# Two cross-attention passes in one kernel: the weighted sums between a step's two blocks of scores

## What is computed

```
q = (queries @ Wq + bq), k = (keys @ Wk + bk), v = (values @ Wv + bv)   # 16 heads of 8
scores = jnp.einsum('bhld,bhsd->bhls', q, k) * SCALE                   # 64 x 6272 a head
weights = jax.nn.softmax(scores, axis=-1)
out = jnp.einsum('bhls,bhsd->bhld', weights, v)
out = out.transpose(0, 2, 1, 3).reshape(B, L, D_MODEL)
out = out @ Wo + bo
```

## Time and profile before

| what | us |
|---|---|
| median of three runs | 349.97 (348.47 to 351.13) |
| the profiled execution | 349.22 |
| its span, first to last instruction | 347.4 |
| PE matmul busy | 305.5 (88%) |
| PE weight loads busy | 208.1 (60%) |
| DVE busy | 223.6 (64%) |
| ACT busy | 168.5 (48%) |
| chain that ended last, on PE | 72% |

### The profile page before, as it was taken

How to read it: one execution, slowest core, us unless ns; L and a number is a source line. 1 busy time by engine, 2 the same in 40 slices (tenths; PEclk the granted TensorE clock), 3 DMA queues, 4 the chain that set the end, 5 groups by cost and what they waited for, 6 DMA issues and landing times.

```text
span 347.4 us, 7751 instructions
## 1 busy us (share of the span) xinstructions
PE 305.5 (88%) x3308; PEld 208.1 (60%) x3308; DVE 223.6 (64%) x452; ACT 168.5 (48%) x224; POOL 30.6 (9%) x22
## 2 busy tenths in 40 slices
PE   2999979999999998998775998999999996647976
PEld 1446747777677774555254665777777775234645
DVE  5588678788875102763996788878878302537653
ACT  2344445556556767593954233655646683012000
POOL 9400000000000012331350000000000000000000
PEclk9999999999999999998899899999999999675999
DMA  7653986544300450201044999954669200000000
GB/s 255 241 113 87 257 185 132 121 93 104 88 2 2 172 219 0 48 15 31 2 91 104 204 347 401 242 130 93 136 222 458 126 2 1 2 0 1 2 0 6
DMA packets 8114, 41.12 MB, mean 118 GB/s; under 512 B 2192, under 2 KB 2512, under 8 KB 7568
## 3 DMA queue, kind: packets, MB, share of 16 engines
q1 hardware_dynamic: 7936, 40.32, 41.1%
q10 hardware_dynamic: 144, 0.31, 0.3%
HBM read 21.32 MB, written 0.03 MB: 61 GB/s over the span
## 4 chain that ended last, share of the span: by engine, by line
PE 72%; DVE 16%; ACT 7%; issue 3%; DMA 1%; POOL 0%; ACTq 0%; DVEq 0%
PE ps L712 71%; ACT prob L342 2%; DVE arena L469 2%; DVE arena L466 2%; DVE mx L441 2%; DVE y L420 1%; DMA consts<-in_const 1%; ACT arena L322 1%; ACT arena L324 1%; DVE arena L475 1%; PE ps L724 0%; PE ps L856 0%; ACT lnv L347 0%; DVE st L416 0%; DVE vaug L701 0%
## 5 line engine op out<-in xcount | busy, mean ns | idle before, releaser
L342 ACT ACTIVATE prob<-ps 128x1024 f32<-128x1024 f32 (+1 forms) x104 | 100.4, 976 | 64.6 <-PE ps L712 64.2
L441 DVE TENSOR_REDUCE mx<-ps 128x1 f32<-128x512 f32 (+1 forms) x156 | 95.2, 655 | 22.8 <-PE ps L712 20.0
L712 PE MATMUL ps<-qst,kst 128*128 128x256 f32 x392 | 71.9, 305 | 2.9 <-DVE qst L436 2.2
L712 PE MATMUL ps<-kst,qst 128*128 128x512 f32 (+1 forms) x208 | 70.6, 416 | 4.4 <-issue 2.9
L712 PEld LDWEIGHTS ps<-qst,kst 128*128 128x128 f32 x392 | 53.8, 188 | 20.4 <-issue 10.1
L712 PE MATMUL ps<-prob,vaug 128*18 128x128 f32 x1568 | 55.8, 274 | 0.0
L712 PEld LDWEIGHTS ps<-kst,qst 128*128 128x128 f32 x208 | 35.4, 189 | 19.9 <-issue 9.3
L712 PEld LDWEIGHTS ps<-prob,vaug 128*18 128x18 f32 x1568 | 40.4, 97 | 11.3 <-issue 8.5
L447 DVE TENSOR_REDUCE mx<-ps 128x2 f32<-128x1024 f32 (+1 forms) x26 | 29.6, 1160 | 7.2 <-PE ps L712 7.1
L307 ACT ACTIVATE vaug<-ps 128x512 f32<-128x512 f32 (+1 forms) x26 | 14.8, 573 | 28.1 <-PE ps L712 27.7
L460 DVE COPY avsb<-ps 128x256 f32<-128x256 f32 x8 | 3.4, 420 | 31.5 <-PE ps L712 31.5
(11 more groups left out here) (190 smaller groups left out, 270.9 us busy)
## 6 DMA issues: line engine op xcount, KB each, us to landing
kst<-arena SPq DMA_DIRECT2D x48, 192.0 KB, 3.2
kst<-arena SPq DMA_DIRECT2D x48, 128.0 KB, 2.4
arena<-in_experts SPq DMA_DIRECT2D x1, 5760.0 KB, 18.6
kst<-arena SPq DMA_DIRECT2D x24, 144.0 KB, 2.7
w<-in_experts SPq DMA_DIRECT2D x1, 3456.0 KB, 11.8
w<-in_late SPq DMA_DIRECT2D x1, 3284.5 KB, 11.5
arena<-in_experts SPq DMA_DIRECT2D x1, 3072.0 KB, 14.3
arena<-in_ctxT SPq DMA_DIRECT2D x2, 768.0 KB, 8.0
```

The lines of the kernel that those rows point to most:

```text
L342: nc.scalar.activation(prob[:, B % PROBS, 0:w], ps[:, b0:b0 + 2, :].rearrange("p a b -> p (a b)")[:, 0:w], ACT.Exp, scale=XSCALE).then_inc ...
L441: V.reduce_max(mx[:, p, k:k + 1], ps[:, bnk, 0:width(k)], AX).then_inc(max_read, 1)
L712: return mm(out_, lhsT, rhs, start=start, stop=stop, skip_group_check=True)
```

## The change

In a step of two blocks, the scores of the first block are now followed by up to two slots, then by the weighted sums of the preceding step, then by the scores of the second block and the rest of the slots. In a step of one block the preceding step's weighted sums now stand first, then the scores and all slots. `gather` and the weights of layer 1 still stand at the end of their step. No other engine's list changes.

```
                     left = list(slots)
-                    for G, i in here:
-                        scores(G, i)
-                        if left:
-                            max_slot(l, left.pop(0))
+                    if len(here) == 2:
+                        scores(*here[0])
+                        for s in left[:2]:
+                            max_slot(l, s)
+                        left = left[2:]
+                    for G, i in before:
+                        weighted(G, i)
+                    scores(*here[-1])
                     for s in left:
                         max_slot(l, s)
-                    for G, i in before:
-                        weighted(G, i)
                     if j == 1 and g >= 1:
                         gather(G0 + g - 1)
```

## The result

The changed kernel took 357.3 us (median of four runs, 354.5 to 360.1) beside 349.3 of the kernel before: a ratio of 1.020, 95% interval 1.015 to 1.025. The longest of the four, 360.1 us, counts as a slow execution and is left out of the ratio; the other three have a median of 356.1. Timed again on another occasion the kernel took 358.5, a ratio of 1.028 (1.024 to 1.031). I had said 354, 350.5 to 356.5, and slower: the sign was right, the size too small by 2 to 4.5 us. The range holds the 356.1, but neither 357.3 nor 358.5. The profiled execution is that longest one (mean granted clock 0.938), so I use it for what happens inside the cross-attentions and have a second profile of the same kernel beside it.

A forecast was written before the change was run, and what follows sets the result against it. Two loops, exponentials and the maxima's banks, were taken to hold full steps near 3.2 us, the banks' remaining after the change. Per layer 0.34 plus 1.9, twice, gave 4.5 us on 349.22 or 349.97: forecast 354, range 350.5 to 356.5.

The forecast's parts named there:

- Two loops: Full cross-attention steps: second block's exponential waiting on a prob buffer (3.20 us) and maxima waiting on three banks (3.19).
- the banks' loop: Full steps: a maximum waits until the bank three slots earlier is read; still 3.19 us a step after the change.
- First steps: Start of layer 0's cross-attention: weighted sums of step [3,4] at 53.26, 1.20 us earlier than before.
- Boundaries: From step [11,12] to the next group's [3,4]: 9.92 us, 1.07 more, with block 0 waiting 0.48 for the accumulator's copy.
- The gather's switch: Four gathers separated from weighted sums: 0.43 instead of 0.23 ahead, already in the sum; another 0.21 each would add 0.8.
- To the last copy: From step [9,10] of group 2 to a layer's last copy: about 22.2 us in layer 1, 1.9 more than 20.34.
- Block 0's wait for its exponential: Group 3: block 0's weighted sums wait for its own exponential, at 7.78 instead of about 7.1, about 0.7 us.
- steps of group 3: Group 3, without maxima: a new loop through each second block's exponential, 2.42 us a step against 2.50.
- The banks' loop not binding: Rival: 18 full steps at 3.06 give back 2.3 us, total 351.6; chance 0.12.
- The exponentials as the whole stall: Rival: waits for exponentials vanish, full steps 3.06, group 3 steps 2.14, total 343; chance 0.06.
- PE full: Rival: order makes no difference, only four gathers' switch is paid, 4 x 0.2, total 350; chance 0.12.
- More late than followed: Rival: third maximum's read slips behind others, 0.17 in each of 18 steps, total 357; chance 0.08.

The follow-up runs named there:

- Short reads: Changed kernel with DVE's reads of the maxima's banks in the slots covering only 128 of 512 columns; ratio to the kernel before 0.996.
- the late maximum: Kernel before with the fourth maximum moved behind the weighted sums in steps [1,2] to [7,8] of groups 0 to 2; 347.5 us, ratio 0.995.
- filled: 35 idle identity products added on PE behind layer 1's last copy: kernel before 346.4 us, changed kernel 352.4, fourth maximum behind the weighted sums 343.1.
- the pause: Kernel before with eight small chained DVE operations (1.7 us) ahead of layer 1's queries; 352.9 us, ratio 1.011.

## Why the prediction was right, and where it was short

*The bound.* Two loops of 3.2, both real. Full steps are 3.19 (I said 3.19), with the wait moved from ACT to the second maximum, as written. Short reads show that the banks' loop is what holds them; with the late maximum they show that 3.06 is PE's own (3.07 and 3.09 measured).

*First steps.* Weighted sums of [3,4] at 53.25; I had 53.26.

*Boundaries.* Weighted sums of [11,12] at 65.64 (65.65), of [3,4] at 75.66 (75.57): 10.02 for 9.92. The copy starts at 71.71, 2.82 behind the scores at 68.89, as worked out. What lacks is small: 0.53 from copy to weighted sums for my 0.47, and 0.03 more for those. The gather's switch costs what the rows said, 0.67 from the pair of maxima to it (73.29 to 73.96; I had 0.66). No further 0.21 is to be seen at the separated gather. The Trainium skill, "TensorEngine Tiling (Array Packing)", Key Properties, which I had set beside that price, says that changing the tiling mode drains TensorE and gives no figure; these rows show nothing beyond what the sum had.

*To the last copy.* 22.50 in layer 1 where I had 22.2; only the spacing from the last weighted sums to the copy is off (298.72 to 299.37, so 0.65 for my 0.4). Block 0's wait for its exponential is 0.84 by the row (I had 0.7), steps of group 3 are 2.42 (2.42), the shift's wait 0.97.

*The sum.* 5.4 for the order where I had 2 x (0.34 + 1.9) = 4.5. Step [9,10] of group 2 comes 0.52 late in layer 0 (107.63 for 107.11; I had 107.45), the rest of the layer takes 22.50 - 20.34 = 2.16 more, and in layer 1 it is the same to 0.1. And then **the step that fell short: I added it to a time in which the clock was as before**. My sum has no term for the stretch behind the cross-attentions, since no instruction of it is touched. It measured 2.4 to 2.7 more in the two profiles of the changed kernel, and 1.5 or more in every other kernel that moved it and was not filled. 5.4 + 1.5 to 2.7 is 6.9 to 8.1, against 7.0 (1.020) and 9.6 (1.028) measured; the rest is put down to the clock in the other stretches, as the starred 1.6 of the first profile and 0.9 in each cross-attention of the second. That the first timing's 356.1 still lay in the range is partly luck: nothing in the range was set aside for the clock, and the second timing lay outside it.

*The rivals.* The banks' loop not binding: refuted, 0.17 of waiting put down to DVE in each full step. The exponentials as the whole stall: refuted by the same row. PE full: refuted by the late maximum, which removed 0.12 to 0.13 a step with the same work. More late than followed, 357: its number came, its mechanism (third reads slipping) did not.

**Open.** Why the clock comes back for 6.8 us in both profiles of the kernel before and in no other profile of an unfilled kernel. In the first of them PE had worked from 297.20 to beyond 300.68 without a gap when the clock rose at 300.7; in the changed kernel the same work, from 305.14, brought no rise. The fall came 2.7 us behind the last copy in both profiles of before and between 1.8 and 4.6 in the others. That it is the place of this work against the clock's changes fits, and the pause supports it, but it is argued and not shown, as is why the kernel before hits it in nearly every execution.

## What to carry to other kernels

When two loops have nearly the same length, opening one gives nothing; write down for each the spacings that it is made of, and look for the gap that the other one shares (here: the weighted sums between two maxima of a ring of three banks, whose length no order with that gap changes). Work moved from the end of a step to its middle loses its cover at the boundaries: ask of the first product behind it what it waits for, as here a copy queued behind three reads. And a sum over untouched code is only as good as the clock in it: 1.7 us of delay cost 3.6.

## What was not expected of the hardware

The granted clock behind the last copy follows the kernel's own waits: 27 to 31 us at 0.50 in eight unfilled kernels, 20.5 in the kernel before, 3.4 to 14 with 35 idle products. The same eight transposes take 1.06 us at one level and 1.92 at the other, the same two score products (four passes) 1.67 and 2.57. The mark of a matmul row at 100% busy hid both loops: 55.70 of 55.70 with 0.15 us of waiting in each step.
